# Attention kernel on one core: values moved between the second and third score, maxima spread over 12 steps and turned in halves, and a 128-column gate product in the last stage

## What is computed

```python
x = x + xattn0(layernorm(x), ctx)          # int8-like rounding of q, wq, o, wp; softmax over 1601 keys
x = x + ffn0(layernorm(x))                 # 512 -> 2048 -> 512, rounded gelu in between
x = x + xattn1(layernorm(x), ctx, mask)    # clipped, masked softmax, then its own layernorm
x = x + ffn1(layernorm(x))
# ffn1(x):
logits = einsum('bsd,ed->bse', x, W_gate)          # 8 experts
top2, _ = top_k(logits, 2)
shared = relu(x @ W_up.T) @ W_down.T
out = shared + sum(softmax(top2)) * (x @ W_expert)
```

## Time and profile before

| | |
|---|---|
| times of three runs | 3014.86, 3014.37, 3011.03 us; median 3014.37 us |
| profiled execution | 3015.58 us, of which 3013.8 us are the span from first to last instruction |
| busy over the span | PE 2687.9 us (89%), PEld 1717.9, DVE 1823.5 (61%), ACT 1303.0 (43%), POOL 1133.2 (38%) |
| mean granted TensorE clock | 0.945 of full speed |
| L827, DVE reduces of the windows | 512 of 989 ns |
| L796, ACT exponentials | 832, mean 597 ns |
| L886, POOL sums | 112, mean 4570 ns |
| L725 scores, L693 windows on PE | 832 and 1024 matmuls |

### The profile page before, as it was taken

How to read it: one execution, slowest core, us unless ns; L and a number is a source line. 1 busy time by engine, 2 the same in 40 slices (tenths; PEclk the granted TensorE clock), 3 DMA queues, 4 the chain that set the end, 5 groups by cost and what they waited for, 6 DMA issues and landing times. The chain is left out here.

```text
span 3013.8 us, 35766 instructions
## 1 busy us (share of the span) xinstructions
PE 2687.9 (89%) x14361; PEld 1717.9 (57%) x14376; DVE 1823.5 (61%) x2480; ACT 1303.0 (43%) x1916; POOL 1133.2 (38%) x305
## 2 busy tenths in 40 slices
PE   6999999969999999999946999976899999993998
PEld 5888888844444444444415777765344333332777
DVE  5353535336666656666436665435699999985654
ACT  4121212104666666666633222222577888872110
POOL 1000000024776767677641000000477777772110
PEclk9999999978999999999978999997899999996899
DMA  6454544363425243342032101015867777703110
GB/s 246 159 192 159 191 160 159 148 162 66 95 58 116 58 100 74 79 95 58 19 120 70 42 1 42 15 33 165 204 149 157 155 156 155 155 20 115 54 43 28
DMA packets 160757, 321.89 MB, mean 107 GB/s; under 512 B 12328, under 2 KB 71752, under 8 KB 160592
## 3 DMA queue, kind: packets, MB, share of 16 engines
q1 hardware_dynamic: 160592, 319.61, 39.0%
HBM read 207.28 MB, written 112.28 MB: 106 GB/s over the span
## 5 line engine op out<-in xcount | busy, mean ns | idle before, releaser
L827 DVE TENSOR_REDUCE win_max<-psum 128x1 f32<-128x802 f32 x512 | 491.8, 989 | 283.8 <-PE psum L693 283.2
L796 ACT ACTIVATE probs<-psum 128x512 f32<-128x512 f32 (+1 forms) x832 | 475.7, 597 | 312.6 <-PE psum L725 302.4
L1613 DVE TENSOR_SCALAR probs<-psum,bound 128x1024 f32<-128x1024 f32 (+1 forms) x416 | 508.1, 1278 | 49.2 <-PE psum L1510 49.1
L886 POOL TENSOR_TENSOR pooled<-pooled,probs 128x2048 f32<-128x2048 f32 x112 | 511.8, 4570 | 68.2 <-ACT probs L796 56.4
L1568 ACT ACTIVATE probs<-probs 128x1024 f32<-128x1024 f32 (+1 forms) x416 | 440.7, 1059 | 119.4 <-DVE probs L1613 83.0
L725 PE MATMUL psum<-q_st,k_st 128*128 128x512 f32 (+1 forms) x832 | 369.6, 453 | 45.3 <-ACT probs L796 31.7
L1648 POOL TENSOR_TENSOR pooled<-pooled,probs 128x2048 f32<-128x2048 f32 x80 | 368.4, 4605 | 79.0 <-ACT probs L1568 79.0
L725 PEld LDWEIGHTS psum<-q_st,k_st 128*128 128x128 f32 (+1 forms) x832 | 150.2, 184 | 319.3 <-ACT probs L796 243.8
L693 PE MATMUL psum<-k_st,q_st 96*128 96x402 f32 x1024 | 291.4, 369 | 31.7 <-DMA q_st<-q_lo 23.4
L1510 PE MATMUL psum<-q_st,k_st 128*128 128x512 f32 (+1 forms) x832 | 250.2, 422 | 14.4 <-DMA q_st<-q_lo 14.4
L1510 PEld LDWEIGHTS psum<-q_st,k_st 128*128 128x128 f32 (+1 forms) x832 | 137.6, 186 | 187.2 <-DVE probs L1613 113.9
(11 more groups left out here) (258 smaller groups left out, 4153.6 us busy)
## 6 DMA issues: line engine op xcount, KB each, us to landing
k_st<-k_hi SPq DMA_DIRECT2D x64, 801.0 KB, 14.8
k_st<-k_lo SPq DMA_DIRECT2D x48, 801.0 KB, 11.1
k_hi<-kt_hi SPq DMA_DIRECT2D x32, 801.0 KB, 3.6
k_lo<-kt_lo SPq DMA_DIRECT2D x32, 801.0 KB, 5.5
v_rows<-v_out SPq DMA_DIRECT2D x96, 256.0 KB
v_st<-v_rows SPq DMA_DIRECT2D x32, 768.0 KB
q_st<-q_hi SPq DMA_DIRECT2D x64, 256.0 KB, 11.2
ctx_raw<-in_ctx_t SPq DMA_DIRECT2D x16, 800.5 KB, 8.0
```

Of the source, the lines that this page charges most:

```text
L796: A.activation(probs[i % NPROBS][0:rows, j, :], bank(score_banks.where["score", u, t, j])[0:rows, :], ACT.Exp, scale=1.0 / ROOT).then_inc( ...
L827: V.tensor_reduce(win_max[:, r, j, c:c + 1], window(windows.where["max", u, i])[:, :, 0:MV], AX.XY, ALU.max).then_inc(max_done, 1)
L886: G.tensor_tensor(pooled[:], before[:], probs[tile(u, POOLED[k]) % NPROBS][:], ALU.add).then_inc(pool_added, 1)
L1613: V.tensor_scalar(probs[i % NPROBS][0:rows, half * W:half * W + W, :], window(("score", u, t, half))[0:rows], bound[0:rows, u // NG, t:t + 1],
```

## The change

In `attention_0`:
- PE's order in a step becomes s0, M0, s1, V (with sums), M1, s2, s3, M2, then closing or turn.
- Windows per step are 2, 2, 3, 3, 3, 2, 3, 3, 3, 2, 3, 3, 0 instead of ten times 3, then 2, 0, 0.
- The turn is made for two heads at a time: the first half on PE behind step 8, the second behind step 12, on DVE one step ahead of each (behind the windows of steps 7 and 11). Each half has its own `max_cols`, four transposes and one ACT copy.
- The rounded copy of the maxima is a `tensor_tensor` maximum of the column with itself instead of a `tensor_copy`.

In the last stage:
- The gate's weights are padded to 128 columns (two memsets on DVE) and become the stationary operand: 12 matmuls of 512 columns a batch instead of 48 of 8 columns. ACT copies the result (`logits_t`), PE transposes it behind `up` 0 (four transposes), DVE reads the best eight from PSUM behind `h_lo` 0, and the steps after it move to `f == 1` (ACT) and `f == 2` (DVE).
- `o_cols` of batch 0 is loaded first, then the projection's weights, bo and rs, the rows, gamma and beta. `o_cols` of later batches are loaded as soon as the ones before have been split, one batch earlier than before.

```diff
-            NQ, NSLOT, NPROBS, LAG, CLOSE_AT, TURN_AT, WINDOWS = 3, 3, 6, 2, 3, 11, 3
+            NQ, NSLOT, NPROBS, LAG, CLOSE_AT = 3, 3, 6, 2, 3
+            TURN_AT = {8: 0, 12: 1}
+            WINDOWS = [2, 2, 3, 3, 3, 2, 3, 3, 3, 2, 3, 3, 0]
+            HALF = HPG * RT
...
 
-                    return range(min(t * WINDOWS, HPG * RT * 2), min((t + 1) * WINDOWS, HPG * RT * 2))
+                    return range(sum(WINDOWS[:t]), sum(WINDOWS[:t + 1]))
...
-                    def turn(u):
-                        slot, free = windows.take(("turn", u))
+                    def turn(u, half):
+                        slot, free = windows.take(("turn", u, half))
                         M.wait_ge(*free)
-                        M.wait_ge(columns, u + 1)
+                        M.wait_ge(columns, 2 * u + half + 1)
                         for r in range(RT):
-                            m = M.transpose(window(slot)[:, 0, r * P:(r + 1) * P], max_cols[:, r, :], ident[:])
+                            m = M.transpose(window(slot)[:, 0, r * P:(r + 1) * P], max_cols[half][:, r, :], ident[:])
                         m.then_inc(turned_ps, 1)
-                        windows.freed_by(turned, 2 * u + 2)
+                        windows.freed_by(turned, 2 * u + half + 1)
...
-                        if coming[1:]:
-                            max_of(*coming[1])
                         if behind:
                             values(*behind)
                             if behind[1] == TT - 1:
                                 last_sum(behind[0])
+                        if coming[1:]:
+                            max_of(*coming[1])
                         if now:
                             scores(*now, 2)
+                        if now:
+                            scores(*now, 3)
                         if coming[2:]:
                             max_of(*coming[2])
-                        if now:
-                            scores(*now, 3)
-                            if now[1] == CLOSE_AT and now[0]:
-                                closing(now[0] - 1)
-                            if now[1] == TURN_AT and now[0] + 1 < UNITS:
-                                turn(now[0] + 1)
+                        if now and now[1] == CLOSE_AT and now[0]:
+                            closing(now[0] - 1)
+                        if now and now[1] in TURN_AT and now[0] + 1 < UNITS:
+                            turn(now[0] + 1, TURN_AT[now[1]])
...
+                    def turn(u, half):
+                        j = 2 * half
+                        A.wait_ge(turned_ps, 2 * u + half + 1)
+                        A.activation(q_st[u % NSLOT][96:128, j:j + 2, :],
+                                     window(windows.where["turn", u, half])[96:128, 0:1, :].to_broadcast([DH, 2, S]),
+                                     ACT.Copy).then_inc(turned, 1)
...
+                    def turn(u, half):
+                        two = slice(2 * half, 2 * half + 2)
+                        top, rest = (max_cols[half][:, :, 96 + 4 * half + i:100 + 4 * half:2] for i in range(2))
+                        V.wait_ge(max_done, max_window(u, HALF * (half + 1)))
+                        s = own.after(V.tensor_reduce(top, win_max[:, :, two, :], AX.X, ALU.max, negate=True))
                         V.wait_ge(own.sem, s)
-                        s = own.after(V.tensor_copy(max_hi[:], max_cols[:, :, 96:104:2]))
+                        s = own.after(V.tensor_tensor(max_hi[:, :, two], top, top, ALU.max))
                         V.wait_ge(own.sem, s)
-                        V.tensor_tensor(max_cols[:, :, 97:104:2], max_cols[:, :, 96:104:2], f32(max_hi[:]),
-                                        ALU.subtract).then_inc(columns, 1)
+                        V.tensor_tensor(rest, top, f32(max_hi[:, :, two]), ALU.subtract).then_inc(columns, 1)
...
-                        if now and now[1] == TURN_AT - 1 and now[0] + 1 < UNITS:
-                            turn(now[0] + 1)
+                        if now and now[1] + 1 in TURN_AT and now[0] + 1 < UNITS:
+                            turn(now[0] + 1, TURN_AT[now[1] + 1])
...
-                wg_hi, wg_lo = weights.add(sbuf, "wg", a["wg_t"], NE)
+                wg_hi, wg_lo = weights.add(sbuf, "wg", a["wg_t"], NE, padded=P)
...
-                        for r in range(RT):
-                            ps = take(("g", b, r))
-                            if r == 0:
-                                M.wait_ge(x_lo_done, (b + 1) * KT)
-                            products(ps[:, 0:NE], of_rows(r, x_hi, x_lo, wg_hi, wg_lo)).then_inc(g_ps, 1)
-                            banks.freed_by(g_read, b * RT + r + 1)
+                        ps = take(("g", b))
+                        M.wait_ge(x_lo_done, (b + 1) * KT)
+                        terms = []
+                        for k in range(KT):
+                            terms += three(wg_hi[:, k, :], wg_lo[:, k, :], x_hi[:, k, :], x_lo[:, k, :])
+                        products(ps, terms).then_inc(g_ps, 1)
+                        banks.freed_by(g_copied, b + 1)
...
+                            if f == 0:
+                                ps = take(("l", b))
+                                M.wait_ge(g_copied, b + 1)
+                                for r in range(RT):
+                                    m = M.transpose(ps[:, r * P:(r + 1) * P], logits_t[:, r * P:(r + 1) * P], ident[:])
+                                m.then_inc(l_ps, 1)
+                                banks.freed_by(top_read, b + 1)
...
-                        next(side, None)
-                        A.wait_ge(e_ready, b + 1)
-                        A.activation(e2[:], e2[:], ACT.Exp).then_inc(e_done, 1)
-                        next(side, None)
+                        if b:
+                            A.wait_ge(l_ps, b)
+                        A.wait_ge(g_ps, b + 1)
+                        A.activation(logits_t[:], bank(banks.where["g", b]), ACT.Copy).then_inc(g_copied, 1)
+                        advance(side, 2)
...
+                            if f == 1:
+                                A.wait_ge(e_ready, b + 1)
+                                A.activation(e2[:], e2[:], ACT.Exp).then_inc(e_done, 1)
...
+                    V.memset(f32(wg_hi[:]), 0.0).then_inc(zeroed, 1)
+                    V.memset(f32(wg_lo[:]), 0.0).then_inc(zeroed, 1)
...
-                        for r in range(RT):
-                            i = b * RT + r
-                            V.wait_ge(g_ps, i + 1)
-                            V.tensor_copy(logits[:, r, :], bank(banks.where["g", b, r])[:, 0:NE]).then_inc(g_read, 1)
-                            V.wait_ge(g_read, i + 1)
-                            s = own.after(V.max(top[:, r, :], logits[:, r, :]))
...
+                        advance(side, 2)
...
+                            if f == 0:
+                                V.wait_ge(l_ps, b + 1)
+                                for r in range(RT):
+                                    m = V.max(top[:, r, :], bank(banks.where["l", b])[:, r * P:r * P + NE])
+                                    if r == RT - 1:
+                                        m.then_inc(top_read, 1)
+                                    else:
+                                        own.after(m)
+                                V.wait_ge(top_read, b + 1)
+                                for r in range(RT):
+                                    m = V.tensor_scalar(e2[:, r, :], top[:, r, 0:2], top[:, r, 0:1], None, ALU.subtract)
+                                    if r == RT - 1:
+                                        m.then_inc(e_ready, 1)
+                                    else:
...
+                            if f == 2:
+                                V.wait_ge(e_done, b + 1)
+                                s = own.after(V.tensor_reduce(total[:], e2[:], AX.X, ALU.add))
+                                V.wait_ge(own.sem, s)
+                                s = own.after(V.reciprocal(inverse[:], total[:]))
...
-                    def load_batch(b):
+                    def load_o(b):
+                        if b:
+                            Y.wait_ge(o_lo_done, b * NG)
                         for g in range(NG):
                             load(o_cols[:, g, :], o_t_1[b * NG + g], o_landed)
+
+                    def load_rows(b):
                         load(rows[:], rows_of(x_mid, b), x_landed)
 
...
+                    load_o(0)
+                    for j in range(NWO):
+                        weights.on_sp(j)
                     load(bo[:], a["bo1"].partition_broadcast(P), rows_given)
+                    load(rs[:], a["rs"].partition_broadcast(P), rows_given)
+                    load_rows(0)
                     load(gamma[:], a["gamma"].partition_broadcast(P), rows_given)
                     load(beta[:], a["beta"].partition_broadcast(P), rows_given)
-                    load(rs[:], a["rs"].partition_broadcast(P), rows_given)
```

(8 more changed lines are left out.)

64 lines of the change are left out of this document (25 added, 39 removed).

## The result

The changed kernel takes 3020.68 us in the median of seven runs (3018.74 to 3022.48), the kernel before, on the same chip, 3011.81 (3006.57 to 3014.86). The ratio is 1.0028, with a 95% interval of [1.0016, 1.0039]: slower by 0.28%. The forecast was 3021.4, range 2988 to 3036. The profiled execution took 3018.74, of which 3017.0 are the span, 3.2 us more than the one before (3015.58).

A forecast was written before the change was run, and what follows sets the result against it. PE was taken to bound both stages, through where it stands still. Attention +22 and last stage -15 gave +7 on the profiled 3015.58 us, 3022.6; the median, 1.2 lower, was 3021.4, range 2988 to 3036.

The forecast's parts named there:

- The unit: Attention, V of step 12 to the next V of step 12: +1.5 us, on 15 units +22 us.
- Steps 10 and 11: Attention: with three windows each, V to V over these two goes from 6.15 to 3.61 and 3.43, +0.89 us.
- End of the unit with the second turn: Attention: one turn copy behind step 12's exponentials gives -1.50 us; the transposes' wait behind step 12 costs +0.3.
- Step 8 to 9: Attention, first half of the turn: V comes at +9.35 instead of +7.2, +2.15 us a unit.
- The closing: Attention: M1 of step 4 no longer waits 0.36 for o_sb, the closing waits some 0.2: -0.35 us a unit.
- The tensor_tensor waits for GpSimd: Attention, rounded copy on DVE: the new form waits for the running POOL sum like the old copy, lasting 1.5 to 2 us.
- The rival of 2989 without the wait: Rounded copy doesn't wait for POOL: -4 us, clock dips go (-6), 2989 with the last stage; chance 18%.
- The order is worth nothing: Attention, PE's order in a plain step: M1 takes over the unhidden weight load from s2, 3.62 us against 3.61.
- Both rivals on it, -17 and +17: Plain attention step 0.1 shorter, load hidden under V (3004, 11%), or 0.1 longer, load paid twice (3038, 9%).
- The clock in the attention: Clock falls, three or four at ends of units, left at nothing; other end -6 us (four times 1.5).
- `projected`'s start in batches 1 and 2: Last stage: about +13.7 behind the gate instead of +16.5 and +18.2, giving -1.5 and -5.7 us with clock losses.
- the first rival's price: Attention without the tensor_tensor's wait for POOL: -4 us, plus -6 for the clock's dips; 2989, chance 18%.

The follow-up runs named there:

- e2: Changed kernel with DVE's turn made of four tensor_reduce instructions, no copy or tensor_tensor: 2983.86 us, 0.9902 of the kernel before.
- e7: e2 with the turn's last operation, the sum of column and rounded copy, as a tensor_tensor instead of a reduce: 3005.47 us, 0.9968 of the kernel before.
- e6: Kernel before with only PE's order in a step changed; windows, turn and last stage as before: 3014.02 us, 0.9999 of the kernel before.
- e5: Kernel before with only the new last stage, the attention as before: 2992.81 us, 0.9932 of the kernel before.
- e10: Changed kernel with o_cols of batches 1 to 3 loaded as late as in the kernel before: 3039.62 us, 1.0084 of the kernel before.
- e3: Changed attention with the old last stage (narrow gate, old loads) of the kernel before: 3039.14 us, 1.0085 of the kernel before.
- e1: Changed kernel with the rounded copy of the maxima made by tensor_copy again, both halves: 3018.29 us, 1.0011 of the kernel before.
- e11: Changed kernel with reduces in the turn, first half behind step 10, logits copied first on ACT, windows rearranged: 2945.65 us, 0.9772 of the kernel before.
- e4: Changed kernel with the windows of before and the turn halves behind steps 11 and 12: 2981.13 us, 0.9888 of the kernel before.

## Why the prediction was right

The mechanisms of the attention came out term by term. The total owes something to luck: the attention lost 3 us more than forecast and the last stage gave 4 to 6 more, and the forecast of +7 hung on the difference of the two.

**Attention, right step by step.** The unit was forecast at +1.5 and is +1.54. Steps 10 and 11: +0.86 measured (+0.89 forecast). End of the unit with the second turn: -1.20 (-1.50 + 0.3). Step 8 to 9: +2.05 (+2.15); without the wait for GpSimd the chain gave +0.70, and e2 measures +0.82. The closing: -0.17 instead of -0.35, the one term off by half; the closing waits 0.25 for the reduce of M1, where 0.2 was assumed, and the slack takes up less than assumed. The stage came out at +25 instead of +22; a fifth dip (1.6) and the first and last units are the rest.

**The tensor_tensor waits for GpSimd.** Without it the forecast would have been below the kernel before. It was argued from one place of another stage, against the steady 0.18 of L836. e2 and e7 show it: the kind of operation waits, whichever place it has, and a reduce doesn't. The rival of 2989 without the wait is what e2 realises (2983.86, with a last stage that gives more than forecast). That the copy stays a wait in the new form was right; the forecast's 1.7 for it (from +3.7 to +5.4) is 1.8 in the trace.

**The order is worth nothing.** Forecast 3.62 against 3.61, measured 3.59 in both; e6 has 0.9999. The load is paid once, at M1 instead of s2. Both rivals on it, -17 and +17, fall.

**The clock in the attention.** Left at nothing, with -6 as the other end. The five dips of the changed kernel are 8 us, four of before 6, and this was right for the changed kernel. That e2 would lose all of them was in the first rival's price, not in e2's expectation.

**Last stage: right direction, two terms mis-sized.** Forecast -15, measured -19.5 in the four batches and -21 by e5. Batch 0 -4.45 (-4.2) and batch 3 -2.2 (-3.7; a store of 5.20 us lengthened the wait and the clock fell, and in e5, without either, it is -4.7). The term that was off is `projected`'s start in batches 1 and 2, put at 13.7 with a clock loss of 1.3 behind it: it is 12.4 and there is no loss, -4.3 and -8.5 instead of -1.5 and -5.7. The forecast let GpSimd's beta sums fall on o_lo 2 and 3; in fact they start at 2872.94, after o_lo has ended (2872.64). TensorE's wait for the logits' copy was put at 2.3 and is 1.97, 2.03 and, behind the long store, 2.98. The start of the stage, put at 0 with bounds -1 and +3, is -2.4 in this pair, but the old order varies by 1.5 by itself and the new one by 2.5, so no run tells it from 0.

**A step that the prediction passed over.** It worked out the gain of the last stage from the wide gate and took for granted that o_cols would be there. e10 shows that the wide gate with the old loads is worth nothing in the sum of the four batches (3039.62 against e3's 3039.14), so the 21 us need the load that was moved one batch earlier, which had no line of its own in the sum. It took the starts of `projected`, 16.5 and 18.2, from the chain without the transfers of o_cols that stand ahead of them there, 3.99 and 4.62 long. The total was right only because both edits came together. How much the early loads would give without the wide gate stays open.

The Trainium skill says in "SBUF — State Buffer", section "Who interferes with whom", that on trn2 a `tensor_reduce` never contends with GpSimd, while a copy, a cast or a `tensor_scalar` may, and a two-input VectorE operation does against GpSimd's reads. The traces agree on each: 0.16 for the reduces under a running sum in e2, 1.52 for the cast in e1, 4.15 against 0.62 for four `tensor_scalar` in batch 0, 1.67 for the two-input operation in e7.

## What to carry to other kernels

A short VectorE operation behind a long GpSimd one may last until that one ends; where it stands ahead of a queue that the matmul engine waits for, rewrite it as a form that doesn't wait (here a reduce), and price the wait by what queues behind it, not by its length. When a slow piece is made fast, look up what its length had hidden, here a load, and give that a line of its own in the sum. Fill the places where the engine waits anyway before the ones that it pays for: in e11 that gave 11 us without removing any work.

## What the runs showed of the hardware

TensorE's clock: in the changed kernel it fell behind the turn of step 8 in five units, every second one from the middle of the attention on. The stretches of one such unit and the next (from, to, then busy us and count of TensorE, its weight loads, VectorE, ScalarE and GpSimd, then the granted clock, DMA share and GB/s):

```profile
1014.00:1050.00 36.00, 33.75 (x195) 17.34 (x196) 22.23 (x26) 21.31 (x39) 22.18 (x5) 1.00 0.57 122
1050.00:1058.00 8.00, 6.79 (x31) 2.50 (x31) 4.59 (x6) 3.19 (x5) 5.23 (x2) 0.79 0.00 0
```

TensorE had stood idle for 0.95 and 0.26 there. V then took 1.94 instead of 1.06 with the granted clock at 0.50, which is 1.2 GHz, from 1055 to 1057. A few tenths in a step can decide between many dips and none: there are 5, 5 and 6 with 5.65 over step 8 to 9 (the changed kernel, e1, e3), and none with 5.44 (e7). At the end of the unit there are 4 and 5 with 4.73 (before, e5), 8 with 4.36 (e6), and none with 4.26 (e4). Nothing in these runs says more on the cause, and it was not tried apart. At 1.6 us each, the dips can add to a small saving or outweigh it, as in e6.
